# High parts split on ScalarE, joint and projection-free tiles reordered, an eight-matmul gate on one core

## The reference

```python
x = _layernorm(x + _L0_attn_ref(x, W))            # scores above the diagonal, triu and zero -> -9e15
x = _layernorm(x + _L0_xattn_ref(x, ctx, ctx, Wq, bq, Wk, bk, Wv, bv, Wo, bo))
x = _layernorm(x + _L0_ffn_ref(x, ..., W_shared, W_expert, W_gate, bias))

# feed-forward
scores = jax.nn.softmax(xf @ W_gate, axis=-1)     # 7 gate columns
expert_weights, _ = jax.lax.top_k(scores, K)      # K = 2, then divided by their sum
...                                               # all tokens meet the one W_expert
out = (shared + moe_out + bias).reshape(b, n, d)
```

## Time and profile before

| | |
|---|---|
| median of 3 runs | 2062.03 us (2056.57 to 2062.41) |
| the profiled execution | 2065.07 us, its span 2063.4 us |
| mean granted TensorE clock | 0.984 |
| PE matmuls | 1981.0 us busy (96%), 9888 matmuls |
| DVE | 1505.2 us busy (73%) |
| ACT | 1123.8 us busy (54%) |
| POOL | 763.0 us busy (37%) |
| self-attention stage | to about 375 us of the span |
| cross-attention stage | from about 387 to about 1820 us |
| feed-forward stage | from about 1823 us on |

### The profile page before, as it was taken

The page is one execution under the profiler, slowest core; times in us unless marked ns, Lnnn a source line. Parts: engine busy times, 40 slices in busy tenths (PEclk is TensorE's granted clock), DMA queues, the critical chain, the costliest instruction groups (busy, mean ns, idle before and its releaser), DMA issues. The chain is left out here.

```text
span 2063.4 us, 29656 instructions
## 1 busy us (share of the span) xinstructions
PE 1981.0 (96%) x9888; PEld 1649.9 (80%) x9888; DVE 1505.2 (73%) x3146; ACT 1123.8 (54%) x2395; POOL 763.0 (37%) x910
## 2 busy tenths in 40 slices
PE   8999999799999999999999999999999999789997
PEld 6877787578888888888888888888888888567776
DVE  6777676477777777777777777777777777678786
ACT  4333333267666666666666666666666666522221
POOL 5344434023333243332333323333333333436662
PEclk9999999999999999999999999999999999899999
DMA  7556666854525445253553625435264353222121
GB/s 285 225 224 233 256 254 240 318 163 147 193 68 194 124 152 184 82 186 114 192 174 112 225 87 190 164 113 184 72 202 148 120 194 103 72 67 82 56 68 61
DMA packets 111222, 326.48 MB, mean 158 GB/s; under 512 B 9056, under 2 KB 9056, under 8 KB 107104
## 3 DMA queue, kind: packets, MB, share of 16 engines
q1 hardware_dynamic: 111072, 324.59, 46.2%
HBM read 207.12 MB, written 83.89 MB: 141 GB/s over the span
## 5 line engine op out<-in xcount | busy, mean ns | idle before, releaser
L917 POOL TENSOR_SCALAR c_prob<-c_prob,all_rden 128x512 f32<-128x512 f32 x512 | 348.3, 693 | 963.0 <-DVE all_rden L1061 963.0
L967 ACT ACTIVATE c_prob<-a_score,all_negmax 128x512 f32<-128x512 f32 x512 | 348.0, 685 | 398.6 <-DVE all_negmax L1055 398.5
L1096 DVE TENSOR_TENSOR c_pt<-a_turned,c_pt 128x512 fp32r<-128x512 f32 x512 | 330.1, 687 | 179.4 <-ACT c_pt L994 175.5
L1055 DVE TENSOR_REDUCE all_negmax<-a_score 128x1 f32<-128x512 f32 x512 | 327.7, 681 | 0.1
L1225 PE MATMUL a_score<-c_ks,c_qs 128*128 128x512 f32 x1024 | 302.3, 416 | 1.1 <-ACT c_prob L967 1.1
L1249 PE MATMUL a_av<-c_pt,c_vs 128*128 128x512 f32 x1024 | 279.9, 395 | 17.2 <-DVE c_pt L1096 17.2
L994 ACT CAST c_pt<-a_turned 128x512 fp32r<-128x512 f32 x512 | 274.0, 587 | 39.5 <-PE a_turned L1236 35.9
L1236 PEld LDWEIGHTS a_turned<-all_ident,c_prob 128*128 128x128 f32 x2048 | 241.8, 141 | 34.2 <-issue 0.6
L1236 PE MATMUL a_turned<-all_ident,c_prob 128*128 128x128 f32 x2048 | 268.4, 274 | 0.0
L1249 PEld LDWEIGHTS a_av<-c_pt,c_vs 128*128 128x128 f32 x1024 | 191.6, 189 | 63.2 <-DVE c_pt L1096 13.0
L1214 PE MATMUL a_proj<-all_third_buffer,all_first_buffer 128*128 128x512 f32 x768 | 187.6, 393 | 12.5 <-SPq L834 11.3
(11 more groups left out here) (167 smaller groups left out, 2764.4 us busy)
## 6 DMA issues: line engine op xcount, KB each, us to landing
all_first_buffer<-ctxT_scratch SPq DMA_DIRECT2D x64, 512.0 KB, 6.9
c_wk<-wk_scratch SPq DMA_DIRECT2D x64, 512.0 KB, 3.9
c_wq<-wq_scratch SPq DMA_DIRECT2D x64, 512.0 KB, 4.8
...
c_ks<-c_ks SPq DMA_DIRECT2D x128, 256.0 KB, 3.3
ctxT_scratch<-s_csp SPq DMA_DIRECT2D x8, 2048.0 KB, 15.4
c_y<-y_steps_scratch SPq DMA_DIRECT2D x16, 1024.0 KB, 5.5
y_steps_scratch<-c_y SPq DMA_DIRECT2D x15, 1024.0 KB, 6.4
```

Of the source, the lines that this page charges most:

```text
L917: nc.gpsimd.tensor_scalar(prob[:, n % 2, i, :], prob[:, n % 2, i, :], rden[:, n % 2, i:i + 1], 1.0, ALU.mult, ALU.mult).then_inc(p_ready, 1)
L967: nc.scalar.activation(prob[:, n % 2, i, :], spsum[:, i % 2, :], ACT.Exp, bias=negmax[:, n % 2, i:i + 1], scale=1.0, accum_out=den[:, n % ...
L1055: nc.vector.tensor_reduce(negmax[:, n % 2, i:i + 1], spsum[:, i % 2, :], AX.X, ALU.max, negate=True).then_inc(smax, 1)
L1096: nc.vector.tensor_tensor(pt[:, t % 2, LO, :], tpsum[:, t % 2, :], as_f32(pt[:, t % 2, HI, :]), ALU.subtract).then_inc(pt_lo, 1)
```

## The change

In self-attention ScalarE takes over the scaling of `wraw` and the high parts (`split_w_hi` at the head of a batch, `split_c_hi` behind the two late pieces of `x1_hi_tile`), and GpSimd keeps the low parts, all behind its scalings of probabilities (`split_lo`). VectorE takes `q_lo_tile(b + 1, 1)` ahead of the layer norm's `scale`. At the joint the last batch's stores move behind the loads of the next stage, `ks` and `op` trade places in memory so that ScalarE's first key no longer waits for `w_stored`, and the last norm is cut in two around a key's low part. In the steps of cross-attention without a projection the two tiles alternate on PE, ScalarE and VectorE where they went in pairs, and the split of the shared weight moves behind the low parts on VectorE. In the feed-forward the gate's high and low weights lie side by side in one 128-column tile, so that a depth tile takes two matmuls and not three; VectorE copies and adds the two halves of the logits (`gate_max`), ScalarE's exponentials read the sum, and `turn_lo` is cut in two around `finish_tile` 2.

```diff
             sp.dma_start(xparts[b - 1], as_f32(x1t[:, :, :, :])).then_inc(x1t_stored, 16)
-        for w in range(NWP):
-            store_w(b, w)
-        store_c(b)
         if b < NB - 1:
+            store_parts(b)
             load_w(b + 1)
...
-        sp.wait_ge(c_stored, 16 * NB)
+        sp.wait_ge(c_stored, 16 * (NB - 1))
         load_ctx(nc, held, cparts, 0)
         sp.wait_ge(s_mm, T * NB)
-        sp.wait_ge(w_stored, 16 * NWP * NB)
+        sp.wait_ge(w_stored, 16 * NWP * (NB - 1))
         load_half(nc, held.third, wparts[2], 0, held.wv_loaded)
...
         sp.dma_start(as_f32(held.second[:, :, :, :]), xparts[0]).then_inc(held.x_loaded, 16)
+        store_parts(NB - 1)
 
     def sync_end():
         sp.wait_ge(y_stored, 16 * NB)
         sp.wait_ge(x1t_stored, 16 * (NB - 1 + K))
+        sp.wait_ge(w_stored, 16 * NWP * NB)
+        sp.wait_ge(c_stored, 16 * NB)
 
...
-            pool.tensor_scalar(wsp[:, w, HI, :], wraw[:, w, :], 1.0, 1.0, ALU.mult, ALU.mult).then_inc(w_hi, 1)
             pool.wait_ge(w_hi, NWP * b + w + 1)
+            if w == 0:
+                pool.wait_ge(w_scaled, b + 1)
             pool.tensor_tensor(wsp[:, w, LO, :], wraw[:, w, :], as_f32(wsp[:, w, HI, :]),
                                ALU.subtract).then_inc(w_lo, 1)
-
-    def split_c(b):
-        pool.wait_ge(craw_loaded, 16 * (b + 1))
-        wait(pool, c_stored, 16 * b)
         for k in range(K):
-            pool.tensor_scalar(csp[:, k, HI, :], craw[:, k, :], 1.0, 1.0, ALU.mult, ALU.mult).then_inc(c_hi, 1)
             pool.wait_ge(c_hi, K * b + k + 1)
...
-            split_w(b + 1)
-            pool.wait_ge(norm.normed, T * b + T)
-            split_c(b + 1)
+        split_lo(b)
...
+    def split_w_hi(b):
+        act.wait_ge(w_loaded, 16 * (b + 1))
+        act.activation(wraw[:, 0, :], wraw[:, 0, :], ACT.Copy, scale=QSCALE).then_inc(w_scaled, 1)
+        act.wait_ge(w_scaled, b + 1)
+        wait(act, w_stored, 16 * NWP * b)
+        for w in range(NWP):
+            act.copy(wsp[:, w, HI, :], wraw[:, w, :]).then_inc(w_hi, 1)
+
+    def split_c_hi(b):
+        act.wait_ge(craw_loaded, 16 * (b + 1))
+        wait(act, c_stored, 16 * b)
+        for k in range(K):
+            act.copy(csp[:, k, HI, :], craw[:, k, :]).then_inc(c_hi, 1)
 
...
     def scalar_batch(b):
+        split_w_hi(b)
         if b:
             x1_hi_tile(b - 1, 2)
             x1_hi_tile(b - 1, 3)
+        split_c_hi(b)
...
+            q_lo_tile(b + 1, 1)
             norm.scale(nc, y, y)
-            q_lo_tile(b + 1, 1)
             q_lo_tile(b + 1, 2)
             q_lo_tile(b + 1, 3)
...
+    WO, ks = sc.sb("WO", [P, 2, PAIRS, D], F32R), sc.sb("ks", [P, 2, 2, 2, S], F32R)
     y, pt = sc.sb("y", [P, T, D]), sc.sb("pt", [P, 2, 2, S], F32R)
...
+    op = sc.sb("op", [P, 2, PAIRS, S], F32R)
     qs = sc.sb("qs", [P, 2, 2, S], F32R)
...
             norm_tile(0, t)
+        pool.wait_ge(before.w_stored, 16 * len(before.wparts) * NB)
...
     def scalar_group(g, u, first, last):
         for step in range(STEPS):
-            for tile in ahead(g, step, last):
-                exp_tile(*tile)
-            name = slot(step, first, last)
-            if name and name[0] != "O":
-                proj_hi_part(g, name, u)
+            name, tiles = slot(step, first, last), ahead(g, step, last)
+            if name:
+                for tile in tiles:
+                    exp_tile(*tile)
+                if name[0] != "O":
+                    proj_hi_part(g, name, u)
+            elif tiles:
+                exp_tile(*tiles[0])
             if step % 2 == 0:
                 for head in head_before(g, step, first):
                     o_first(*head)
             pt_hi_tile(g, 2 * step)
+            if tiles and not name:
+                exp_tile(*tiles[1])
...
         proj_hi_part(-1, "V0+", 1)
         before.norm.root(nc, NB - 1)
-        act.wait_ge(before.w_stored, 16 * len(before.wparts) * NB)
...
     def vector_group(g, u, first, last):
         for step in range(STEPS):
-            for tile in ahead(g, step, last):
+            name, tiles = slot(step, first, last), ahead(g, step, last)
+            for tile in tiles if name else tiles[:1]:
                 max_tile(*tile)
             if step:
                 finish_slot(g, u, step - 1, first, last)
             else:
                 proj_lo_part(g - 1, SLOTS[-1], 1 - u)
-            for tile in ahead(g, step, last):
+            for tile in tiles if name else tiles[:1]:
                 recip(*tile)
             if step % 2 == 0:
                 for head in head_before(g, step, first):
                     o_second(*head)
+            if tiles and not name:
+                max_tile(*tiles[1])
+            pt_lo_tile(g, 2 * step)
+            if tiles and not name:
+                recip(*tiles[1])
+            pt_lo_tile(g, 2 * step + 1)
             if last and step in WS_AT:
                 k = WS_AT.index(step)
                 dve.wait_ge(held.ws_hi, k + 1)
                 nc.vector.tensor_tensor(held.second[:, LO, k, :], held.x2[:, 1, k, :],
                                         as_f32(held.second[:, HI, k, :]), ALU.subtract).then_inc(held.ws_lo, 1)
-            pt_lo_tile(g, 2 * step)
-            pt_lo_tile(g, 2 * step + 1)
...
     def tensor_group(g, u, first, last):
         for step in range(STEPS):
-            for tile in ahead(g, step, last):
-                scores(*tile)
-            name = slot(step, first, last)
+            name, tiles = slot(step, first, last), ahead(g, step, last)
             if name:
+                for tile in tiles:
+                    scores(*tile)
                 bank_free(g, name, first)
                 project(g, name, u)
-            for t in (2 * step - 2, 2 * step - 1):
-                if step:
-                    values(g, t, u)
-                elif not first:
-                    values(g - 1, TILES + t, 1 - u)
-            turn(g, 2 * step)
-            turn(g, 2 * step + 1)
+                for t in (2 * step, 2 * step + 1):
+                    values_before(g, u, first, t)
+                for t in (2 * step, 2 * step + 1):
+                    turn(g, t)
+            else:
+                for e, t in enumerate((2 * step, 2 * step + 1)):
+                    if tiles:
+                        scores(*tiles[e])
+                    values_before(g, u, first, t)
+                    turn(g, t)
...
-        graw, G = sc.sb("graw", [P, K, P]), sc.sb("G", [P, 2, K, P], F32R)
+        graw, G = sc.sb("graw", [P, K, PAD]), sc.sb("G", [P, K, P], F32R)
...
+                        nc.scalar.activation(e[:, i, :NG], lsum[:, i, :NG], ACT.Exp, bias=gneg[:, i:i + 1], scale=1.0,
                                              accum_out=den[:, i:i + 1]).then_inc(e_done, 1)
...
                                         ALU.subtract).then_inc(x2_lo, 1)
 
                 def gate_max(b):
                     dve.wait_ge(lt_mm, done(b + 1))
-                    v.tensor_reduce(gneg[:, :], logit[:, :, :NG], AX.X, ALU.max, negate=True).then_inc(g_max, 1)
+                    v.tensor_copy(llo[:, :, :], logit[:, :, PAD:2 * PAD]).then_inc(g_low, 1)
+                    dve.wait_ge(g_low, b + 1)
+                    v.tensor_tensor(lsum[:, :, :], logit[:, :, :PAD], llo[:, :, :], ALU.add).then_inc(g_sum, 1)
+                    dve.wait_ge(g_sum, done(b + 1))
+                    v.tensor_reduce(gneg[:, :], lsum[:, :, :NG], AX.X, ALU.max, negate=True).then_inc(g_max, 1)
 
                 def route_weights(b):
...
                         norm2.scale(nc, x2[:, nu], x2[:, nu])
                     finish_tile(b, u, 1)
+                    if more:
+                        turn_lo(b + 1, nu, range(0, 2))
                     finish_tile(b, u, 2)
                     if more:
-                        turn_lo(b + 1, nu)
+                        turn_lo(b + 1, nu, range(2, K))
...
                     pe.wait_ge(gate_out, done(b))
-                    three_pass(nc, gateT[:, :], lambda s, k: G[:, s, k, :], lambda m, k: x2T[:, u, m, k, :],
-                               K).then_inc(gate_mm, 1)
+                    for k in range(K):
+                        for m in (HI, LO):
+                            ins = nc.tensor.matmul(gateT[:, :], G[:, k, :], x2T[:, u, m, k, :],
+                                                   start=(k == 0 and m == HI), stop=(k == K - 1 and m == LO))
+                    ins.then_inc(gate_mm, 1)
```

51 lines of the change are left out of this document (28 added, 23 removed).

## The result

The changed kernel takes **2013.29 us** (median of 4 runs, 2012.24 to 2014.81) where the kernel before took 2061.66 beside it: a ratio of 0.9771, 95% interval 0.9754 to 0.9788, 48.4 us less. The forecast was 2001. The direction was right and the size 12 us too large; 0.9771 of the 2062.03 from which the prediction started is 2014.8, just past the range's upper end of 2014. The profiled execution took 2012.89 us (span 2011.2; before 2065.07 and 2063.4).

What follows compares the result with a forecast made beforehand. PE was taken as the bound in nearly every stretch, so its stops count. Terms -29.6 - 3.4 - 13.5 - 6.3 - 8.3 = -61.1 us take 2065.07 to 2004.0; less 3.04 to the runs' median, 2001 us, range 1989 to 2014.

Steps and rivals of the forecast that it cites:

- Self-attention and start: Splits no longer beside the norm or VectorE's first splits, second low q tile earlier: -29.6 us and, at the start, -3.4.
- the second low q tile's place: Self-attention: taking it ahead of the norm's four scalings saves PE's smaller wait, 0.4 us a batch, 2.8 us in all.
- Rival (1): Self-attention: exponentials become the bound, 1.4 us more on ScalarE reaches PE seven times; +10, 2011 us, chance 0.14.
- (3): Self-attention: low parts slip by 7 us or more and meet the norm again; 27 us given back, 2028 us, chance 0.05.
- (4): Batch heads: ScalarE waits for `w_loaded` with everything queued behind it; slower, 2092 us with landing 20 us late, chance 0.02.
- Joint: Between self-attention and the first scores: PE's wait for SP and part of the rest go, -13.5 us (bounds -7 and -15).
- at most 11.4 + 3.5 = 14.9 us go ... I take -13.5: Joint: 11.4 us before "V0+", 3.5 of slow clock and key wait, less something for stores sharing the queues.
- rival (2): Joint: stays bound by transfers, stores hold up x or the doubled key by 7 us; 2008 us, chance 0.13.
- between steps whose projections cover it: 0: First group of cross-attention: alternating in its four empty slots gains and loses nothing net; 0 us, bounds -2 and +3.
- (5): Cross-attention and joint: alternating steps bring nothing and the clock sinks in the joint; 2009 us, chance 0.06.
- Last group: Cross-attention's steps 9 to 15: alternating and later weight splits give -6.3 us, with -6.4 from steps 14 and 15.
- Feed-forward: Shorter gates -7.3, low turned parts moved -3.6, copy and add +2.6: together -8.3 us (bounds -3 and -12).

Runs made afterwards that it cites:

- the run with the later low parts: The changed kernel with GpSimd's four low parts of the context waiting, in batches 0 to 6, until the sums of values are done; 2050.45 us.
- The three orders of the transfers: The changed kernel with the joint's doubling first, then also the weights' stores behind it, then key weights, doubling, y, stores; 2012.31, 2010.3 and 2007.57 us.

## Why the prediction was right or wrong

**Self-attention and start: right.** Contention is the cause (27.0 us for the splits against the 27.1 forecast), the start is exact (-3.4), and the second low q tile's place gives 4.3 and not 2.8, since a wait of 0.31 us costs 0.62 from start to start. Rival (1), exponentials as the new bound, did not happen: the first comes at 77.03, 0.44 us ahead of the value tiles, where the earlier trace rows had it 1.27 ahead, so it is 0.83 us late against PE's tiles (1.2 forecast), and PE has no wait for a low value tile. An exponential again starts 0.02 us behind its table load of 1.28 us. The Trainium skill, "ScalarE: Activation LUTs", section "What ACT_TABLE_LOAD costs", adds a drain of about 1.38 us to that; the trace doesn't agree, and the measurement decides. Rivals (3) and (4) did not occur; the run with the later low parts shows how near (4) was, with ScalarE waiting for a load at the head of six batches.

**Joint: the term was too large.** Its first part was right, the 11.3 us before "V0+" went whole. The step that failed is "at most 11.4 + 3.5 = 14.9 us go ... I take -13.5", where the last batch's 4 MB of stores were named as sharing the queues and then priced at 1.4 us. That was rival (2): 8.4 us gained and 6.41 us of new wait, together the 14.9 of the sum. The three orders of the transfers show that the bytes ahead of the doubling are the cause. They also show that it is not the stores alone: with all 4 MB still ahead, and only the key weights and y (1.5 MB) moved behind it, the wait is 1.52 us; with 2 MB (the context's store) or 2.5 MB (that and the key weights) ahead it is gone. The change lost another 1.4 us net in the next stage for the slower clock behind the stop: 2.7 us over the first 16 matmuls, less 1.3 that a wait of 0.83 us had cost there from start to start and no longer costs. What could have been worked out from the rows: 4 MB at the 433 GB/s that the queues moved behind the old stop (386.8 to 391.8 us of the kernel before) are 9.7 us. Issued some 15 us ahead of the doubling, they would just have been through by themselves, but the loads of x, of the key weights and the store of y go through the same queues ahead of it, 3.5 MB more.

**First group: the step that failed is "between steps whose projections cover it: 0".** A projection covers work that is needed behind it. The second score tile of such a step stands ahead of its projection, and that tile needs the very exponential which alternation had put off. The 5.6 us are the 1.4 of the clock behind the joint and 4.2 of alternation, and pairs give 5.2 us back, 1 more than alternation's, because the clock did not fall in that stretch. The bounds of -2 and +3 were too narrow, and no rival joined this with the joint: rivals (2) and (5) stood at 2008 and 2009, and what both describe happened.

**Last group: right size, wrong reason.** The forecast of -6.3 laid -6.4 on steps 14 and 15, "without new tiles, VectorE no longer blocks and the two tiles overlap", as a fruit of alternating. The block was VectorE's wait for ScalarE's high part of the shared weight, ahead of the low parts. Moving it is worth 8 us and more, and alternation took some 2 of that back. The sum came out only because both edits are in it.

**Feed-forward: right.** -8.8 against -8.3. A batch takes 27.09 us (27.1 forecast); the turned parts gave 4.4 where I had 3.6, and the copy and the add cost PE 0.51 us a batch (0.71 - 0.20) where I had 0.44; none of the new instructions was held by GpSimd's scalings, which run from 1846.85 while the copy takes 0.19 us and the add 0.19. The clock at the stage's start differs between kernels that are alike there: from the first turned tile to the first product it is 9.2 us in some and 10.5 in others. From that tile to the end the stage takes 221.0 to 222.3 us in them, so up to 1.3 us of that term is chance.
